# Spectral stage of a conv and attention hybrid: the next image pair's transposes moved ahead of the last mixing, its first convolution ahead of the direct taps, the last pair written out

## What is computed

```python
def _stu_conv(phi, u, n):
    ...
    Vf = jnp.fft.rfft(phi, n=n, axis=0)
    Uf_p = jnp.fft.rfft(u, n=n, axis=1)
    Uf_m = jnp.fft.rfft(u * sgn3, n=n, axis=1)
    U_plus = jnp.fft.irfft(Vf[None, :, :, None] * Uf_p[:, :, None, :], n=n, axis=1)[:, :sl]
    U_minus = jnp.fft.irfft(Vf[None, :, :, None] * Uf_m[:, :, None, :], n=n, axis=1)[:, :sl]
    U_minus = U_minus * sgn[None, :, None, None]
def _compute_spectral(u, sigma, phi, Mpp, Mpm):
    U_plus, U_minus = _stu_conv(phi, u, PADDED_SL)
    s = sigma ** SIGMA_POW
    out = jnp.einsum('btkd,k,kde->bte', U_plus, s, Mpp)
    out = out + jnp.einsum('btkd,k,kde->bte', U_minus, s, Mpm)
...
...
def _compute_ar_u(Mu, u):
    sl = u.shape[1]
    out = jnp.zeros(u.shape[:2] + (Mu.shape[-1],), dtype=u.dtype)
    for i in range(Mu.shape[0]):
        ui = jnp.pad(u, ((0, 0), (i, 0), (0, 0)))[:, :sl]
        out = out + jnp.einsum('btd,de->bte', ui, Mu[i])
    return out
...
for i, frac in enumerate((1, 2, 4, 8)):
    xi = x[:, :T // frac]
    si = _stu(xi, sigma, phi, M_u[i], M_phi_plus[i], M_phi_minus[i])
```

## Time and profile before

| | |
|---|---|
| median of 3 runs | 2935.61 us (2935.15 to 2936.2) |
| the profiled execution | 2933.56 us, of which the traced span is 2931.8 us |
| TensorE busy in the span | 2741.8 us (94%), 18761 matmuls |
| VectorE, ScalarE, GpSimd busy | 2185.6 us (75%), 1330.1 us (45%), 1740.8 us (59%) |
| spectral stage | from about 2268 us to the end of the span |
| chain of work that ended last, by line | TensorE L1535 15% of the span, L1550 4%, L1579 1% |
| mean granted TensorE clock | 0.967 of full speed |

### The profile page before, as it was taken

The page is one execution under the profiler, slowest core; times in us unless marked ns, Lnnn a source line. Parts: engine busy times, 40 slices in busy tenths (PEclk is TensorE's granted clock), DMA queues, the critical chain, the costliest instruction groups (busy, mean ns, idle before and its releaser), DMA issues. The chain is left out here.

```text
span 2931.8 us, 60696 instructions
## 1 busy us (share of the span) xinstructions
PE 2741.8 (94%) x18761; PEld 1789.2 (61%) x18761; DVE 2185.6 (75%) x3909; ACT 1330.1 (45%) x1788; POOL 1740.8 (59%) x1831
## 2 busy tenths in 40 slices
PE   3639999999999999999999999999998899999998
PEld 1335655655655655656655655655655788888887
DVE  3448788788788788788888888888886675767676
ACT  1103444444444444444444444444443465656565
POOL 3746777777777777777777777777776670000000
PEclk8659999999999999999999999999999899999999
DMA  5542222222222222222222212244443553444343
GB/s 151 145 112 59 64 63 62 64 63 58 68 63 58 68 63 58 64 67 58 65 67 58 65 54 69 65 64 60 64 65 55 161 168 116 147 130 146 116 154 105
DMA packets 159644, 249.21 MB, mean 85 GB/s; under 512 B 71662, under 2 KB 93502, under 8 KB 159582
## 3 DMA queue, kind: packets, MB, share of 16 engines
q1 hardware_dynamic: 125902, 155.61, 18.8%
q0 software_dynamic: 33680, 92.71, 13.1%
HBM read 230.65 MB, written 17.04 MB: 84 GB/s over the span
## 5 line engine op out<-in xcount | busy, mean ns | idle before, releaser
L1083 ACT ACTIVATE attention_probs<-attention_pss 128x1024 f32<-128x1024 f32 x576 | 590.1, 1024 | 310.7 <-PE attention_pss L920 298.4
L1286 POOL DMA_INDIRECT attention_gat<-table,attention_idx x585 | 558.5, 955 | 200.0 <-issue 121.3
L920 PE MATMUL attention_pss<-attention_kq 64*128 64x512 f32 (+3 forms) x3072 | 651.8, 483 | 0.0
L1149 DVE TENSOR_REDUCE attention_mx_half<-attention_pss 128x2 f32<-128x1024 f32 (+3 forms) x520 | 513.2, 1020 | 98.5 <-PE attention_pss L920 98.5
L1022 PE MATMUL attention_psY<-attention_probs,attention_xt 128*64 128x512 f32 (+3 forms) x3120 | 574.1, 496 | 0.2 <-issue 0.2
L1642 DVE SCALAR_TENSOR_TENSOR spectral_eo<-spectral_psE,kept_sig,spectral_eo 64x512 fp32r<-64x512 f32 x512 | 384.0, 750 | 170.1 <-ACT spectral_eo L1617 163.9
L1243 POOL TENSOR_TENSOR attention_kq<-attention_tA,attention_tB 128x512 f32<-128x512 f32 x260 | 416.1, 1611 | 111.0 <-DVE attention_tB L1159 101.7
L1535 PE MATMUL spectral_psE<-spectral_tz,spectral_up 128*128 128x512 f32 (+1 forms) x2304 | 462.1, 358 | 5.8 <-DVE spectral_up L1633 5.8
L1617 ACT ACTIVATE spectral_eo<-spectral_psE,kept_sig 64x512 fp32r<-64x512 f32 x512 | 350.2, 684 | 243.9 <-PE spectral_psE L1535 238.9
L920 PE MATMUL attention_pss<-attention_rows_m,attention_ones 64*128 64x512 f32 (+2 forms) x1536 | 458.8, 530 | 0.0
L1535 PEld LDWEIGHTS spectral_psE<-spectral_tz,spectral_up 128*128 128x128 f32 x2304 | 386.5, 189 | 78.2 <-issue 6.2
(11 more groups left out here) (192 smaller groups left out, 3199.0 us busy)
## 6 DMA issues: line engine op xcount, KB each, us to landing
spectral_tz<-phis SPq DMA_DIRECT2D x128, 320.5 KB, 4.6
spectral_tz<-phis SPq DMA_DIRECT2D x128, 320.0 KB, 4.2
attention_xb<-xn SPq DMA_DIRECT2D x132, 256.0 KB, 3.8
attention_gat<-table,attention_idx POOLq DMA_INDIRECT x585
table<-front_pixT SPq DMA_DIRECT2D x32, 288.0 KB
attention_wt<-in_w SPq DMA_DIRECT2D x66, 128.0 KB, 3.6
attention_xt<-xt SPq DMA_DIRECT2D x18, 128.0 KB, 2.1
attention_xs<-in_x SPq DMA_DIRECT2D x65, 32.0 KB
```

The source lines that it names most:

```text
L920: ins = pe.matmul(out(n), left(rows), right(rows), **flags)
L1083: act.activation(probs[:, u[1], :, :].rearrange("p n q -> p (n q)"), pss[:, slot, :], ACT.Exp, scale=float(E) ** -0.5).then_inc(s_act, 1)
L1149: ins = dve.tensor_reduce(mx[:, :, i] if i < 4 else mx_half[:, :, i - 4, k0 // 4], scores, AX.X, ALU.max)
L1286: pool.indirect_dma_start(gat[:, n, :, :].rearrange("p q c -> p (q c)"), None, d.table.rearrange("r q c -> r (q c)"), bass.IndirectOffsetO ...
```

## The change

TensorE, ScalarE and VectorE each get two functions: begin(n), the transposes and reversing products of pair n with their copies, and pair(g, more), the rest of a pair. begin(0) stands ahead of the loop; begin(g + 1) is issued on TensorE between mix_in(14) and mix_in(15) of pair g, on ScalarE ahead of the copy to low, on VectorE ahead of fin. conv(0) of a pair now stands ahead of its direct taps. The loops run over three pairs, and the fourth is written out behind them, without a begin or a norm for a next pair. On VectorE the first begin also stands ahead of the mixing weights. GpSimd's copy to traw waits for mix_in(0) of the running pair and no longer for mix_in(15). The loop of SyncE's queue is not touched.

```diff
@@ gpsimd @@
-                    pool.wait_ge(s_mix, KF * g + (KF + 2))
+                    pool.wait_ge(s_mix, KF * g + 3)
                     raw(2 * g + 3)
@@ tensor @@
-                pe.wait_ge(s_perm, 17)
-                pe.wait_ge(s_mixu, 32)
-                with pe.Fori(0, G) as g:
+                def begin(n):
+
+                    pe.wait_ge(s_un, 2 * n + 2)
+                    for t in range(NT):
+                        if t % 4 == 0:
+                            pe.wait_ge(s_lo, 64 * n + (t // 4 + 1))
+                        ins = pe.transpose(psE[:, t // 4, (t % 4) * P:(t % 4) * P + P],
+                                           un[:, t].rearrange("p b c -> p (b c)"), m.ident[:, :])
+                    ins.then_inc(s_uTps, 1)
+                    for p in range(2):
+                        pe.wait_ge(s_lo, 64 * n + (p + 3))
+                        for a in range(4):
+                            for x in range(2):
+                                ins = pe.matmul(psE[:, 2 + p, a * P:(a + 1) * P], perm[:, p, x, :],
...
+                    ins.then_inc(s_upps, 1)
+
+                def pair(g, more):
...
-                    pe.wait_ge(s_un, 2 * g + 2)
-
-                    pe.wait_ge(s_lo, 64 * g + 4)
...
+                    pe.wait_ge(s_uT, g + 1)
+                    pe.wait_ge(s_up, g + 1)
+                    pe.wait_ge(s_upl, g + 1)
+                    conv(0)
 
                     pe.wait_ge(s_fin, g + 1)
-                    pe.wait_ge(s_uT, g + 1)
...
-                    pe.wait_ge(s_up, g + 1)
-                    pe.wait_ge(s_upl, g + 1)
-                    for k in range(KF):
+                    for k in range(1, KF):
                         conv(k)
-                        if k:
-                            mix_in(k - 1)
+                        mix_in(k - 1)
+                    if more:
+                        begin(g + 1)
                     mix_in(KF - 1)
+
+                pe.wait_ge(s_perm, 17)
+                pe.wait_ge(s_mixu, 32)
+                begin(0)
+                with pe.Fori(0, G - 1) as g:
+                    pair(g, True)
+                pair(G - 1, False)
@@ scalar @@
-                        if k == STD_AT:
+                        if more and k == STD_AT:
                             std_of(act, g + 2)
-                    act.wait_ge(s_mix, KF * g + KF + 2)
+                    if more:
+                        begin(g + 1)
+                    act.wait_ge(s_mix, KF * g + (KF + 2))
                     act.activation(low[:, :], acc[C:P, :], ACT.Copy).then_inc(s_low, 1)
@@ vector @@
-                            norm(dve, (g + 1) % G, g + 1, LN_AT[k])
+                            norm(dve, g + 1, g + 1, LN_AT[k])
+                    if more:
+                        begin(g + 1)
                     dve.wait_ge(s_low, g + 1)
...
+                for part in LN_AT.values():
+                    norm(dve, 0, 0, part)
+                do = Chain(dve, s_mixing0)
+                begin(0)
+                dve.wait_ge(s_mw[0], 64)
+                weights(dve, do, 0, 0)
```

More of the change, by code:

```diff
@@ L1515, in _ @@
             def _(pe):
-                pe.wait_ge(s_perm, 17)
-                pe.wait_ge(s_mixu, 32)
-                with pe.Fori(0, G) as g:
+                def begin(n):
[11 more added lines that the diff above has]
+                                ins = pe.matmul(psE[:, 2 + p, a * P:(a + 1) * P], perm[:, p, x, :],
+                                                un[:, 2 * a + x].rearrange("p b c -> p (b c)"), start=(x == 0), stop=(x == 1))
+                    ins.then_inc(s_upps, 1)
+                def pair(g, more):
                     def conv(k):
@@ L1592, in _, with begin, pair @@
                                               skip_group_check=True)
-                    pe.wait_ge(s_up, g + 1)
-                    pe.wait_ge(s_upl, g + 1)
-                    for k in range(KF):
+                    for k in range(1, KF):
                         conv(k)
-                        if k:
-                            mix_in(k - 1)
+                        mix_in(k - 1)
+                    if more:
+                        begin(g + 1)
                     mix_in(KF - 1)
+                pe.wait_ge(s_perm, 17)
[4 more added lines that the diff above has]
+                pair(G - 1, False)
             @block.scalar
             def _(act):
-                std_of(act, 1)
-                with act.Fori(0, G) as g:
-                    act.wait_ge(s_uTps, g + 1)
+                def begin(n):
+                    act.wait_ge(s_uTps, n + 1)
                     act.activation(uT[:, 2:2 + S], psE[:, 0:2, :].rearrange("p a n -> p (a n)"), ACT.Copy).then_inc(s_uT, 1)
-                    act.wait_ge(s_upps, g + 1)
+                    act.wait_ge(s_upps, n + 1)
                     act.activation(up[:, 0, :, :, :].rearrange("p a b n -> p (a b n)"),
                                    psE[:, 2:4, :].rearrange("p a n -> p (a n)"), ACT.Copy).then_inc(s_up, 1)
+                def pair(g, more):
                     for k in range(KF):
@@ L1619, in _, with begin @@
                             ins.then_inc(s_hi, 1)
-                        if k == STD_AT:
+                        if more and k == STD_AT:
                             std_of(act, g + 2)
-                    act.wait_ge(s_mix, KF * g + KF + 2)
+                    if more:
+                        begin(g + 1)
+                    act.wait_ge(s_mix, KF * g + (KF + 2))
                     act.activation(low[:, :], acc[C:P, :], ACT.Copy).then_inc(s_low, 1)
+                std_of(act, 1)
+                begin(0)
+                with act.Fori(0, G - 1) as g:
+                    pair(g, True)
+                pair(G - 1, False)
             @block.vector
             def _(dve):
[L1627 to L1632, removed]
+                def begin(n):
+                    dve.wait_ge(s_up, n + 1)
                     dve.tensor_tensor(up[:, 1, :, :, :].rearrange("p a b n -> p (a b n)"),
@@ L1646, in _ @@
                             ins.then_inc(s_lo, 1)
-                        if k in LN_AT:
-                            norm(dve, (g + 1) % G, g + 1, LN_AT[k])
+                        if more and k in LN_AT:
+                            norm(dve, g + 1, g + 1, LN_AT[k])
+                    if more:
+                        begin(g + 1)
                     dve.wait_ge(s_low, g + 1)
@@ L1658, in _ @@
                     ins.then_inc(s_fin, 1)
+                for part in LN_AT.values():
+                    norm(dve, 0, 0, part)
+                do = Chain(dve, s_mixing0)
+                begin(0)
+                dve.wait_ge(s_mw[0], 64)
+                weights(dve, do, 0, 0)
+                with dve.Fori(0, G - 1) as g:
+                    pair(g, True)
+                pair(G - 1, False)
 def program(nc, a, out):
```

10 lines of the change are left out of this document (removed).

## The result

The changed kernel takes 2966.35 us (median of 4 runs, 2963.97 to 2968.2), the kernel before 2935.9 us (4 runs beside them): 1.0102 times as long, 95% interval 1.009 to 1.0115. The forecast was 2968, between 2958 and 2977. The profiled execution took 2967.58 us with a span of 2965.6; against the profiled one of before that is +34.0 us, against the medians +30.4, since executions of one kernel differ by some 4 us.

What follows compares the result with a forecast made beforehand. TensorE's own order of work was taken to bound the kernel. Turns 31.7 plus clock 5.5 less start 5.1 gave +32.1 us, so 2965.7 for the profiled execution and 2968 for the median, range 2958 to 2977.

Steps and rivals of the forecast that it cites:

- the three terms: Over the whole kernel: turns 31.7 us and clock 5.5 us lost, start 5.1 us gained, +32.1 us in all.
- the turn: At three turns between pairs, conv(0) waits for filter 0 with the taps behind it: 31.7 us lost in all.
- the clock: Behind each turn's wait the granted clock falls and slows TensorE: 3 x 1.82 = 5.5 us lost.
- the start: Ahead of the first pair's conv(0), VectorE's earlier begin shortens TensorE's wait from 5.84 to 2.7 us: 5.1 us gained.
- The mechanism: At each turn filter 0's load, queued behind fin and the store, loses the taps' cover: TensorE waits 14 to 15 us.
- The chain from there to conv(0): From the end of mix_in(15): copy to low, fin, store, four loads of filter 0; 14.37 us, unchanged.
- the row: Profile row at the stage's start: 72 matmuls took 16.17 us instead of 14.35 under a fallen clock, 1.82 us.
- the clean carry to the end: The first pair's gain of 5.1 us enters the forecast sum in full.
- The first rival: At the turns, the loads of filter 0 do not hold conv(0): -11.7 us, 2924; 3 in 100.
- The third rival: In the first pair GpSimd's weights become the bound, shrinking the start's gain: up to 2973; 8 in 100.

Runs made afterwards that it cites:

- load_ahead: The changed kernel with the next pair's filter 0 loads issued ahead of the wait for fin and of the store on SyncE's queue: 2920.43 us, ratio 0.9949.
- taps_first: The changed kernel with conv(0) behind the direct taps again, everything else as changed: 2940.45 us, ratio 1.0016.
- keep_warm_unrolled: The changed kernel with 118 extra transposes behind mix_in(15) of the first three pairs and TensorE's pair loop written out: 2960.93 us, ratio 1.0085.
- load_ahead_late_start: The load_ahead kernel with VectorE's first begin behind the mixing weights again: 2933.97 us, ratio 0.9993.
- start_only: The kernel before with only VectorE's first begin moved ahead of the mixing weights: 2934.72 us, ratio 0.9994.
- keep_warm_longer: The changed kernel with 118 extra transposes on TensorE behind mix_in(15) of the first three pairs, loop kept: 2972.29 us, ratio 1.0124.
- start_fetch_early: The start_only kernel with GpSimd's second-round weight loads issued as soon as the first have landed: 2930.73 us, ratio 0.9984.

## Why the prediction was right

- **The sum.** On the traces the three terms came to 30.4 + 6.3 - 3.8 = 32.9 us against 32.1. That it is so close is in part luck: the turn was 1.3 us too dear, the clock 0.8 too cheap and the start 1.3 too good, and these errors nearly cancel. The medians differ by 30.4, the two profiled executions by 34.0.
- **The mechanism** was right, and shown both ways: with the load moved ahead the loss becomes a gain (load_ahead), and with the taps back ahead of conv(0) most of it goes (taps_first). The queue's order, which the change does not touch, made the difference.
- **The turn.** begin was put at 4.76 us and took 4.37, and it starts 0.16 us ahead of the end of mix_in(14), so mix_in(15) ended 3.0 us later and not 3.59. The chain from there to conv(0) was put at 14.37 and was 14.37, 14.35 and 14.68. Waits and moves together were put at 31.7 us and came to 36.7 - 6.3 = 30.4.
- **The clock** was put at 3 x 1.82 = 5.5 us. conv(0) was 2.56, 2.06 and 1.64 us above 7.29, 6.3 in sum, and keep_warm_unrolled, which fills the wait, is 5.4 us below the changed kernel. The Trainium skill, "TensorE: Matmul & The Clock Gate", section "HAM oscillation — how this bites in real kernels", prices such a fall at half the throttled time, which the prediction put at 2.1 us a turn, 6.2 in all. The traces agree with it as well as with the row.
- **The start** was put at -5.1 us. It is -4.6 at mix_in(0) and -3.8 at the turn. The step that was too simple is the clean carry to the end: GpSimd's loads came later (its queue waited 1.17 us for VectorE) and TensorE waited 0.6 us for a filter table that was loaded while GpSimd's third round of loads ran; that these held it up is not shown. mix_in(4) kept 1.3 us of slack (weights done at 2345.64, used at 2346.90), where 2.1 were forecast. The 4.6 us are the gain on the kernel before, where the taps ran during the wait. With conv(0) ahead of the taps a late first begin costs far more, 13.5 us in load_ahead_late_start.
- **The first rival** (the load does not hold conv(0)) was priced at 2924. load_ahead made it true on purpose and measured 2920.4; the turns gained 2.6, 3.4 and 3.8 us, since begin was shorter and the 'issue' gaps were under 1.5 us.
- **The third rival** did not happen in the changed kernel, and did in start_only (0.8 us) and taps_first (0.6 us).

## What to carry to other kernels

When work is moved ahead of other work on the busiest engine, look up what each moved piece reads and when that lands: cover that costs nothing may be all that hides a transfer. A queue's in-order stream with a wait in it (here a load behind a store behind the last addition) has to be moved with the consumer; with it, the same reordering was 0.5% faster, without it 1.0% slower. And a saving measured in one order of work does not carry to another: 4.6 us at the start against a kernel whose taps covered part of the wait, 13.5 where nothing did.

## What the hardware showed unexpectedly

- **A loop's back edge took 4.4 to 4.6 us beside a DMA burst.** On TensorE it took 1.59 us in the kernel before, at a turn where the DMA engines were idle (share 0.00), and 1.45 and 0.97 in load_ahead, likewise. In keep_warm_longer it came beside the burst of filter loads (share 0.72 in the gap) and was 4.43 and 4.61 us; with the loop written out 0.75 and 0.92 were left, which were a wait for the load. The Trainium skill, "Runtime: NRT & Kernel Launch", section "Instruction fetch mechanics", says that a branch out of the fetched window stalls for a DMA of the target. The traces agree that the branch is what costs, and do not show the fetch itself. That the burst makes it dearer is argued from these numbers and not shown apart: the loop of keep_warm_longer is also 118 instructions longer, and no run has that loop's branch at a quiet moment.
- **The granted clock can fall behind short gaps, and gaps of one length do not always do it.** In start_only it went to 0.50 behind 1.17 and 2.15 us, and behind 1.17 and 2.11, with a mixing step of 2.12 or 2.13 us between; in start_fetch_early it stayed at 1.00 behind 1.17 and 2.13 with 2.11 between. At the start it fell behind 2.65 us in load_ahead and stayed up behind 2.66 in the changed kernel:

```profile
2290.69 8.82 PE L1559 MATMUL spectral_psE<-spectral_tz,spectral_up 128*128 128x512 f32 x36 [2.65 <-DVE spectral_up L1659]
...
2293.00:2294.00 1.00, 1.00 (x5) 0.81 (x4) 0.96 (x2) 0.42 (x1) 0.92 (x2) 0.50 0.00 0
```

  Which of the two happens depends on more than the gap's length, and no run here settles on what. It moved the time by about 1 us at a turn and 1.5 at the start, so differences of that size between single executions say nothing about an edit.
